# Cross-attention with a mixture of experts: first steps rearranged, centroid products in three groups

## What is computed

```python
# block 1: queries from the normalised x, keys and values from context and x
q = lat @ Wq;  k, v = split(concat([norm(ctx), lat]) @ Wkv)
attn = softmax(q @ k.T * scale);  x = x + (attn @ v) @ Wout
# block 2: routing by centroids, one expert per row
assign = argmax(z @ centroids.T);  xn = layer_norm(z) * ln_g[e] + ln_b[e]
h = relu(xn @ w1[e].T + b1[e]);  y = z + h @ w2[e].T + b2[e]
out = a * y + (1 - a) * z          # a = sigmoid(z @ centroids[e]);  z = norm(x)
```

## Time and profile before

| | |
|---|---|
| median of three runs | 1070.82 us |
| profiled execution, its own time | 1071.78 us |
| its span | 1070.0 us |
| TensorE matmul busy | 99% of the span |
| VectorE (DVE) / ScalarE (ACT) / GpSimd (POOL) busy | 75% / 63% / 46% |
| mean granted TensorE clock | 0.996 |

### The profile page before, as it was taken

The page is one execution under the profiler, slowest core; times in us unless marked ns, Lnnn a source line. Parts: engine busy times, 40 slices in busy tenths (PEclk is TensorE's granted clock), DMA queues, the critical chain, the costliest instruction groups (busy, mean ns, idle before and its releaser), DMA issues.

```text
span 1070.0 us, 24078 instructions
## 1 busy us (share of the span) xinstructions
PE 1056.2 (99%) x8454; PEld 945.2 (88%) x8454; DVE 798.6 (75%) x1907; ACT 670.3 (63%) x1820; POOL 495.2 (46%) x641
## 2 busy tenths in 40 slices
PE   8899999999999999999999999999999999999998
PEld 6789898989888888889898988888898999999997
DVE  7876888888888988888888988798886554444441
ACT  6765757575856767665757576676655646666551
POOL 2653554646464545555464646455454343222222
PEclk9999999999999999999999999999999999999999
DMA  6475676675857566767657585756467657766670
GB/s 208 99 185 135 168 188 165 168 188 141 218 137 200 150 180 157 192 165 189 169 154 196 145 219 137 199 140 156 95 162 222 250 179 267 233 225 228 226 259 30
DMA packets 159660, 190.51 MB, mean 178 GB/s; under 512 B 17453, under 2 KB 149037, under 8 KB 154672
## 3 DMA queue, kind: packets, MB, share of 16 engines
q1 hardware_dynamic: 155088, 179.09, 61.3%
q0 software_dynamic: 3360, 8.53, 2.2%
q10 hardware_dynamic: 1088, 1.31, 0.3%
HBM read 65.72 MB, written 46.07 MB: 104 GB/s over the span
## 4 chain that ended last, share of the span: by engine, by line
PE 94%; DVE 2%; POOL 1%; DMA 1%; ACT 1%; issue 1%; SPq 0%; POOLq 0%; ACTq 0%; DVEq 0%
PE psum L694 16%; PE psum L727 16%; PE psum L869 12%; PE psum L764 11%; PE psum L854 10%; PE psum L743 9%; PE psum L779 9%; PE psum L713 8%; PE psum L782 1%; POOL prob L1677 1%; DMA prob_t<-prob 1%; DVE neg_max L1291 0%; POOL w_o_lo L1731 0%; ACT prob L1037 0%; PE psum L794 0%
## 5 line engine op out<-in xcount | busy, mean ns | idle before, releaser
L1677 POOL TENSOR_TENSOR prob<-prob,inv_sum 128x512 f32<-128x512 f32 x176 | 182.8, 1053 | 203.0 <-DVE inv_sum L1297 202.3
L1037 ACT ACTIVATE prob<-psum,neg_max 128x256 f32<-128x256 f32 x352 | 164.5, 481 | 48.6 <-DVE neg_max L1291 39.6
L1291 DVE TENSOR_REDUCE neg_max<-psum 128x2 f32<-128x512 f32 x256 | 162.3, 673 | 36.5 <-PE psum L743 36.5
L869 PE MATMUL psum<-w,v_n 128*128 128x256 f32 x608 | 134.2, 379 | 0.0
L1303 DVE STREAM_TRANSPOSE prob<-prob 128x512 f32<-128x512 f32 x176 | 121.5, 699 | 9.3 <-POOL prob L1677 8.9
L869 PEld LDWEIGHTS psum<-w,v_n 128*128 128x128 f32 x608 | 114.2, 190 | 14.8
L1677 POOL TENSOR_TENSOR w_ring<-w_ring,inv_sum 128x512 f32<-128x512 f32 x76 | 78.2, 1042 | 78.4 <-DVE inv_sum L1297 78.0
L1044 ACT ACTIVATE head_out_hi<-psum 128x512 fp32r<-128x512 f32 x52 | 31.1, 598 | 114.3 <-PE psum L764 91.7
L1748 POOL DMA_INDIRECT out<-x_in,r_ring x38 | 39.8, 1048 | 127.0 <-DVE x_in L1535 126.7
L1027 ACT ACTIVATE v_n<-psum 128x512 f32<-128x512 f32 x128 | 78.3, 612 | 20.7 <-PE psum L727 20.7
L1016 ACT ACTIVATE k_hi<-psum 128x512 fp32r<-128x512 f32 x128 | 77.2, 604 | 18.1 <-PE psum L694 16.8
(11 more groups left out here) (185 smaller groups left out, 2712.6 us busy)
## 6 DMA issues: line engine op xcount, KB each, us to landing
sorted_rows<-filler SPq DMA_DIRECT2D x54, 660.0 KB, 5.0
prob_t<-prob SPq DMA_DIRECT2D x176, 128.0 KB, 2.8
w_ring<-prob SPq DMA_DIRECT2D x176, 128.0 KB
w<-in_experts SPq DMA_DIRECT2D x19, 1024.0 KB
w_ring<-in_experts SPq DMA_DIRECT2D x18, 1024.0 KB, 5.6
prob_t<-w_ring SPq DMA_DIRECT2D x76, 128.0 KB, 2.8
w_ring<-w_ring SPq DMA_DIRECT2D x76, 128.0 KB
w_ring<-normed SPq DMA_DIRECT2D x56, 128.0 KB, 3.0
```

Source lines behind the costliest of these rows:

```text
L869: last = pe.matmul(bank[:, 0:d_model], hid[:, s % 2, f, i * P:(i + 1) * P], w2[:, f * d_model:(f + 1) * d_model], start=(f == 0), stop=(f ...
L1037: act.activation(prob_at(u, bb)[:, :, parity, i], scores_i, ACT.Exp, bias=neg_max[:, at, i:i + 1], accum_out=prob_sum[:, at, i:i + 1]).the ...
L1291: dve.tensor_reduce(neg_max[:, (4 * u + n) % 8, :], psum[:, n, :].rearrange("p (i j) -> p i j", i=2), AXIS_X, ALU.max, negate=True).then_i ...
L1677: pool.tensor_tensor(probs, probs, inverse, ALU.mult).then_inc(s_soft, 1)
```

## The change

It moves work on five queues and changes two items in form.

- DVE: the statistics of pair 1 go one by one: two before step 0's maxima, one at the end of step 0, one behind step 1's maxima. The low part of V_REST moves from the end of step 0 to behind the first two maxima of step 1. The statistics of pair 2 move from the end of step 2 to step 3, two behind each low part of the keys.
- POOL: `split_w_out` is made in four parts (`W_OUT_PIECES`), one after step 0's softening, two after step 1's, one after step 2's. The scales of pairs 1 and 2 move between the softening of halves 1 and 2 of steps 1 and 3.
- ACT: `normalise(1)` moves from the middle of step 1 to its end.
- TensorE: the centroid products move from the end of step 4 to directly behind its scores, in groups of 3, 3 and 2 chunks with the keys between them; the column sums belong to the last. The readers on ACT and DVE and the order of banks move accordingly.
- SP: the load of w_out_t moves ahead of the move of (3, 0).

```diff
@@ bank_order
+        if u == 4:
+            order += [("cent",)]
         if following:
             order += [("k", u + 1, 0), ("k", u + 1, 1)]
...
-        if u == 4:
-            order += [("cent",)]
@@ SP
+                    if u == 3:
+                        load_w_out_t()
                     if u < n_steps:
                         move_probabilities(u, 0)
...
-                    if u == 3:
-                        load_w_out_t()
@@ TensorE
+                    if u == 4:
+                        cent_bank = begin(("cent",))
+                        pe.wait_ge(s_const, 4 * 16)
+                        pe.wait_ge(s_wo_t, 2 * 16)
+                        centroid_products(cent_bank, range(0, 3))
                     if following:
                         keys(u + 1, 0)
+                        if u == 4:
+                            centroid_products(cent_bank, range(3, 6))
                         keys(u + 1, 1)
+                    if u == 4:
+                        centroid_products(cent_bank, range(6, HC))
@@ ACT
-                    if u == 1:
-                        normalise(1)
+                    if u == 4:
+                        high_centroids()
...
-                    if u == 4:
-                        high_centroids()
+                    if u == 1:
+                        normalise(1)
                     if u > 0:
                         high_outputs(u - 1)
@@ DVE
                 low_queries(0)
+                layer_norm_stats(1, 0)
+                layer_norm_stats(1, 1)
...
                     maxima(u, 1)
...
+                    if u == 1:
+                        low_weights(V_REST)
...
                     maxima(u, 3)
+                    if u == 1:
+                        layer_norm_stats(1, 3)
...
                         low_keys(u + 1, 0)
+                    if u == 3:
+                        layer_norm_stats(2, 0)
+                        layer_norm_stats(2, 1)
...
                         low_keys(u + 1, 1)
+                    if u == 3:
+                        layer_norm_stats(2, 2)
+                        layer_norm_stats(2, 3)
+                    if u == 4:
+                        low_centroids()
...
                     if u == 0:
-                        low_weights(V_REST)
-                    if u in (0, 2):
-                        for j in range(4):
-                            layer_norm_stats(u // 2 + 1, j)
+                        layer_norm_stats(1, 2)
@@ POOL
-                def split_w_out():
-                    pool.wait_ge(s_wo, 16)
+                def split_w_out(i):
+                    chunks = slice(i * HC // W_OUT_PIECES, (i + 1) * HC // W_OUT_PIECES)
...
                     soften(u, 1)
+                    if u == 1:
+                        layer_norm_scales(1)
+                    if u == 3:
+                        layer_norm_scales(2)
...
                     soften(u, 3)
                     if u == 0:
-                        layer_norm_scales(1)
+                        split_w_out(0)
                     if u == 1:
-                        split_w_out()
+                        split_w_out(1)
+                        split_w_out(2)
+                    if u == 2:
+                        split_w_out(3)
```

More of the change, by code:

```diff
@@ L35 @@
 NW, NW2, NR = 2, 3, 4
+W_OUT_PIECES = 4
 def bank_order(n_pairs, last_of_early, n_early, n_slots):
@@ L539, in load_w_out_t @@
                     sp.wait_ge(s_wlo, len(pieces))
-                    sp.wait_ge(s_wo_split, 2)
+                    sp.wait_ge(s_wo_split, 2 * W_OUT_PIECES)
                     for h in range(2):
@@ L784, in wout, with centroid_products @@
                     last.then_inc(s_job, 1)
-                def centroid_products():
-                    bank = begin(("cent",))
-                    pe.wait_ge(s_const, 4 * 16)
-                    pe.wait_ge(s_wo_t, 2 * 16)
-                    for c in range(HC):
+                def centroid_products(bank, chunks):
+                    for c in chunks:
                         h, at = divmod(c * P, half)
@@ L795, in centroid_products @@
                                       start=(k == 0), stop=(k == KC - 1))
+                    if HC - 1 not in chunks:
+                        return
                     for k in range(KC):
@@ L913, in _ @@
                         layer_1_plain()
-                    if u == 4:
-                        centroid_products()
                     if u == 5:
-                        pe.wait_ge(s_wo_split, 2)
+                        pe.wait_ge(s_wo_split, 2 * W_OUT_PIECES)
                         wait_read(pe, ("cent",))
@@ L1605, in _ @@
                         dve.wait_ge(s_const, 4 * 16)
-                    if u == 4:
-                        low_centroids()
                     if r == 0 and g >= 2:
@@ L1723, in scatter @@
                         in_=row_ring[:, b % NROW, :], in_offset=None).then_inc(s_scat[b % NROW], 16)
-                def split_w_out():
-                    pool.wait_ge(s_wo, 16)
-                    hi, lo = [w[:, :, 0:d_model] for w in w_o]
-                    w = w_o_raw.rearrange("p (c n) -> p c n", c=HC)
+                def split_w_out(i):
+                    chunks = slice(i * HC // W_OUT_PIECES, (i + 1) * HC // W_OUT_PIECES)
+                    if i == 0:
+                        pool.wait_ge(s_wo, 16)
+                    hi, lo = [w[:, chunks, 0:d_model] for w in w_o]
+                    w = w_o_raw.rearrange("p (c n) -> p c n", c=HC)[:, chunks]
                     pool.tensor_copy(hi, w).then_inc(s_wo_split, 1)
-                    pool.wait_ge(s_wo_split, 1)
+                    pool.wait_ge(s_wo_split, 2 * i + 1)
                     pool.tensor_tensor(lo, w, hi, ALU.subtract).then_inc(s_wo_split, 1)
@@ L1769, in _ @@
                         row_scales(2 * g - 1)
-                    if r == 3 and g + 2 < n_pairs:
+                    if r == 3 and 1 <= g < n_pairs - 2:
                         layer_norm_scales(g + 2)
```

## The result

The changed kernel takes 1074.23 us (median of seven runs, 1071.47 to 1076.24) against 1070.98 of the kernel before on the same chip (1069.14 to 1073.68). The ratio is 1.0028, 95% interval 1.0014 to 1.0041: it is slower by some 3 us. The forecast was 1066.1, with a range up to 1069.4; what happened is the case that had 4%, the clock that falls at the new wait and doesn't come back among the groups.

A forecast was written before the change was run, and what follows sets the result against it. TensorE's stream, busy 1056.2 of 1070.0 us, was taken as the bound. Lead 3.9, less 2.1 of new wait, plus 0.9 for products and 2.0 for clock gives 4.7 us won: 1066.1 us, range 1063.7 to 1069.4.

The forecast's parts named there:

- the case that had 4%: Rival "Slower", 4%: clock falls at the new wait and stays down among groups interrupting the keys; 1073.6 us if lasting.
- Lead at step 4's scores: TensorE, steps 1 to 3: shortened chains let step 4's scores start at 63.5 instead of 67.38 us, lead 3.9 us.
- 0.6 told: TensorE, step 2: normalise(1)'s new place delays k_lo, so the values wait 0.6 us (from 0 to 1.5).
- by the row's ratio of 1.4 it loses 0.2 us: DVE, step 1: w_lo meets 0.4 us of POOL's first split part and loses 0.2 us, inside 0.8 us to spare.
- my chain: Step 2's last move lands at 60.9 us, then exponentials, q_hi and exponentials take 2.6 us until step 4's scores.
- The new wait: TensorE, before step 4's first products: stands 2.1 us for the load of w_out_t; bounds nothing to 3.2.
- the order of transfers is kept: SP: w_out_t's load, behind step 2's last move and the fill, lands 11.2 us after the trigger, at 67.3 us.
- The products: 0.9 us won: TensorE, step 4: 36 product records take 4.1 us in three groups instead of 5.0.
- the clock: 2.0 won: TensorE, behind the products: without a fall, outputs take 1.90 instead of 3.61 us, the next scores 1.70 instead of 1.98.
- I expect no fall: Step 4: with groups of 12 records between keys of 1.5 us each, the granted clock stays up.
- the fall at the wait among the rivals: Rival, 22%: clock falls at the new wait before narrow products; 1069.3 us at the earlier 3.2 us price, 1067.7 at half.
- No wait before the queries: TensorE, step 4: products' bank is read by 74.8 us, queries need it at 75.5; no wait, 0.7 us to spare.

The follow-up runs named there:

- the kernel with the groups late: The changed kernel with the three product groups behind step 4's first values, queries and second values, readers at the step's end; 1065.45 us, ratio 0.9946 to the kernel before.

## Why the prediction was wrong, by its steps

**Lead at step 4's scores: 3.9 predicted, 3.1 to 3.2 shown.** The waits came as told: none before the values of step 1, 0.56 before those of step 2 (0.6 told). Before the scores of step 2 it was 1.2 us instead of 0.7, so the lead there is 2.3 us (43.25 less 41.80, with 0.83 of late start given back), not 2.9. The step that failed there is "by the row's ratio of 1.4 it loses 0.2 us": the low part lost 0.66. The Trainium skill (SBUF — State Buffer, Who interferes with whom), which I had turned down, says that a DVE instruction with two SBUF inputs contends with a reading GpSimd instruction for a lock that is held for a whole instruction, and the other blocks. By that rule the trace agrees: POOL's w_o_lo had 0.81 us left, and DVE lost 0.66. The last move of step 2 then starts 0.8 us later than told, once the late start is taken off (57.70 less 0.83 against 56.1). But mending that step would not have given the forecast lead. With the loss taken away the move is issued from 56.21 us, and still the scores of step 4 start at 64.03 and not at 63.5: they stand for ACT's v_n, which comes behind the exponentials and was not in my chain. And I credited the parts of w_out's split with part of the lead, where the runs show no gain from them.

**The new wait: 2.1 predicted, 3.2 shown.** The step that failed is "the order of transfers is kept", from which I took that the move behind the load doesn't touch it. TensorE came 1.56 us later than told (66.76 instead of 65.2) and the trigger 1.6 us later (57.70 instead of 56.1), which cancel; what is left is the landing, 12.15 us behind the trigger and not 11.2. Of that 0.9 us the fill has 0.4 (it landed 5.2 us after its issue, 4.8) and the load behind it the rest. With a move ahead, the load's second half took 5.5 us with only x_cols behind it and 7.2 with the fill; it took 8.3 with the fill ahead and the move behind. By 5.5 against 7.2 us, a transfer that comes after takes its share while the load is under way. The Trainium skill (DMA: Bandwidth & Descriptors, Two DMAs through the same engine are not ordered) has it that descriptors of one queue start in order but are pipelined; the mixed packets agree. What the move behind the load costs it by itself was not measured.

**The products: 0.9 us won, predicted; and the clock: 2.0 won.** They are right as one sum, in kernels that have no wait there: step 4 lasts 17.46 us before, and 14.56 or 14.57 where the clock stays up, with the block or with late groups. That is 2.9 us less, my 0.9 and 2.0 together. The groups have no part in it: block and groups give the same. The old block, which I had at 5.0 us, lasts 5.1 to 5.2 by the earlier trace rows (76.04 to the outputs), with half level in it; at full clock a block takes 4.0.

**The clock: "I expect no fall".** This is the step that turned the sign. I had argued from narrow products (groups with keys between are no long narrow stretch) and put the fall at the wait among the rivals, because waits of 1.6 and 1.3 us had not brought it. The new wait was forecast at 2.1 us, longer than either, so these rows said nothing on whether the clock would stay up behind it. The runs: a wait of 3.3 us brought the clock down even before wide matmuls, and with it filled the groups run at full clock. For the price I had 3.2 us, or half of it, from the length of the fall before. In the profile it was 5.1 (half of 10.2). That narrow work behind the wait makes it longer fits the profiles and the medians, but the length of a single fall is not explained: it was 3.4, 6.8, 10.2 or 13.7 us. The Trainium skill (TensorE: Matmul & The Clock Gate, HAM oscillation) describes a kernel in which waits of 3 to 5 us for a DMA between bursts send the clock down each time. The trace agrees at 3.2 and 3.3 us; here it fell at 1.4 and 1.86 us too, which those waits do not cover. With falls at waits on both sides of 2.1 us, the fall to which I had given 22% and 4% was no side case even at the wait that I forecast.

**No wait before the queries: 0.3 shown.** I had reckoned the products' readers, 0.7 us in time; the wait is one of counting, above.

**The sum, put right.** In the prediction's terms the profiled run has 2.3 of lead, less 3.2 of wait and 0.3 before the queries, plus 2.9 for products and outputs, less 5.1 of clock: -3.4 us, where its span is 3.3 longer. Against the kernel with the groups late (1065.45, measured beside other runs of the kernel before) the changed kernel pays 3.2 of wait, 5.1 of clock and 0.3 before the queries, 8.6 us, which makes 1074.1; it takes 1074.2. With the lead of 3.1 and the longer wait alone the sum would still have been 2.5 us faster: the sign flipped because a wait had been priced at its length, without the clock behind it.

## What to carry to other kernels

A wait that a change gives to TensorE is priced at its length and at the clock behind it: ask what stands behind the wait, since in these runs the clock cost less, in the median, where wide matmuls followed than where narrow ones did. Of two places for work that depends on a transfer, the later one with independent work ahead is worth more than an early one that is free on paper; here it was 8.8 us. And when work changes places, look whether anything numbers items by their place in a list: an item that is finished in another order than listed makes readers wait for the wrong one.

## What was not expected of the hardware

- A wait of 1.86 us before wide matmuls was followed by 3.4 us of half level, while the wait of 1.6 us in the earlier trace rows was not; one of 1.4 us ahead of narrow groups was followed by 13.7 us of it in one run, and five of twelve runs of that kernel were 5 us longer.
- By the mean clocks, the same block of narrow products brought the clock down in most runs of a kernel and left it up in one, 3.0 us faster than the median.
- The same kv_t_lo operation on DVE took 0.97 us when it began with 0.42 us of POOL's kv_t_lo left, and 1.77 us with 1.23 left; the profiles of kernels that are equal up to there start step 0's scores between 17.61 and 18.45 us.
